# Attention kernel: normalisation of half of the tokens moved from the stretch ahead of the second attention into its first pair

## The chip, the cores and the metric

One core of a Trainium2 chip runs one program. The metric is the device time of one execution in microseconds (us). TensorE's matmuls are called PE here, its weight loads PEld, VectorE is DVE, ScalarE is ACT, GpSimd is POOL, and SP is the engine that issues most DMAs.

## The reference

The input is x, 16 batches of 100 tokens of 256 numbers, and a context of 16 x 361 x 256. Two layers follow each other, each a gated cross attention and a gated mixture of eight experts:

```python
x = x + tanh(g_xattn[0]) * L0_xattn(layernorm(x), ctx, ctx, mask)
x = x + tanh(g_ffn[0])   * L0_ffn(layernorm(x))          # 8 experts, top 2, capacity
x = x + tanh(g_xattn[1]) * L1_xattn(layernorm(x), ctx, ctx, mask)
x = x + tanh(g_ffn[1])   * L1_ffn(layernorm(x))          # 8 experts, top 2
```

`layernorm` is (x - mean) / sqrt(variance + 1e-5) over the 256 numbers of a token. The change concerns the one that stands at the head of the third line: the normalised x is the query input of the second attention (16 heads of 64).

## The kernel before

The program has four stages in a row: the first attention (`a_`), the first experts (`f_`, function `experts_first`), the second attention (`b_`, function `attention_second`), the second experts. x lies in SBUF as 100 partitions x (16 x 256); `T["xn"]` is a second tile of that size, and `T["xn_t"]` the transposed normalised tokens, 128 partitions x 2 x 1600.

**The stretch ahead of the second attention.** The tokens come in four quarters of four batches. For each quarter q the code has these pieces:
- `load_back` (SP): the experts' rows come back by DMA, the first share into xn, the second into `xe` (quarters 0 and 1) or the weight buffer `w` (quarters 2 and 3).
- `scale_second(act, q)` (L1997): ACT multiplies the second share by its weight, four activations of 100x256.
- `combine(dve, q)`: DVE adds the first share times its weight to x (L2006, four instructions), then the second share (L2011), and then calls `centre.average`: four `bn_stats` (L1871) and four `bn_aggr` (L1874).
- `centre.scales(pool, q)`: four small POOL instructions (L1882 to L1885) make 1/sqrt(variance) and the shift.
- `centre.apply(act, q)`: ACT writes the normalised quarter into xn, four activations (L1892).
- `centre.turn(pe, bank, q, k)`: PE transposes it (L1900), four transposes for each of k = 0, 1; `turn_rows(q)` calls it for both, into the score banks.
- `keep_rows(q)`: ACT copies both banks of 400 columns to `xn_t` (L865).

Beside this the stretch makes keys (K), values (V) and queries (Q) of batches 0 and 1 in units, the list `pre`: 8 K, 6 V, 8 Q. A Q unit is two matmuls (L639, each shows as two in the trace), a cast on ACT (L808) and a subtraction on DVE (L898). The Q units of `pre` read only quarter 0 of `xn_t`. Units go through three PSUM banks in turn: unit u waits until unit u-3 has been taken. Before the first pair PE waits for all rows kept, for all memsets (semaphore `zeroed`, the last is POOL's memset of the probability tile) and for all units taken:

```python
            pe.wait_ge(rows_kept, DK * Centre.GROUPS)
            pe.wait_ge(zeroed, 8)
            for k in taken.values():
                pe.wait_ge(k.sem, k.before(k.pre))
            iterations(pe, steps)
```

**The pairs.** `iterations` runs eight pairs of batches; pair 0 is written out ahead of a loop. A pair has eight steps p = 0 to 7 of four heads. In each step PE makes scores for four heads (L698), the transposes of the probabilities of the step before (L708, one PSUM bank that ACT empties at L827), the values product of the step before that (L730), and in between the units of `second_schedule`. DVE takes the four maxima (L960), inverts sums and multiplies (L968, L973), and takes units; ACT does the exponentials (L819), copies (L827) and takes units (L808, L795). DVE, ACT and PE run their own written order, so what an engine does between two heads holds up what is queued behind it.

The schedule has four units of kinds W (output projection, step 2), N (step 5), G (step 6) and C (step 7) that work on the pair before (their last field is -1). In pair 0 there is no pair before: PE passes over them and only counts (`no_outputs`), and DVE calls `count_taken`. Pair i makes the queries of pair i+1, so quarter 1 of `xn_t` is read from pair 1's steps on, and quarters 2 and 3 later still.

SP loads contexts during the pairs; a load waits for POOL's `split_context` (L551, L554) of the context before.

## Time and profile before

| | us |
|---|---|
| median of 3 runs | 1506.0 |
| lowest and highest of them | 1504.61, 1637.23 |
| the profiled execution, its own time | 1506.07 |
| its span, first to last instruction | 1504.3 |
| second attention's eight pairs, from 648 on, about | 592 |
| the stretch 605 to 648 ahead of it | 43 |

A profile row of the timeline reads: start in us from the span's start, length in us, engine, source line, operation, output <- input, shapes, count, and in brackets how long the engine was idle before it and who released it. Where PE is busy all the time, the time is PE's; where it idles, the releaser in the brackets names what was late.

### The profile page before, as it was taken

The numbers are of one execution on the slowest core, as the hardware profiler recorded it, in microseconds if no ns is written. First come the engines' busy times: TensorE is split into PE (matmuls) and PEld (weight loads), VectorE is DVE, ScalarE is ACT, GpSimd is POOL, SyncE is SP. The second block draws the span as 40 slices with busy tenths as digits, with TensorE's granted clock in tenths as the row PEclk, the third lists the DMA queues.
The fourth block names the chain that finished last, engine by engine and source line by source line (L and its number), as shares of the span: only waits on it lengthen the run. The fifth ranks groups of instructions, "written<-read, shape, count | busy, mean of one in ns | idle before, by whom it ended". The sixth has DMA issues, their size and how long they took to land. (4 is left out here: it accounts for less than half of the span.)

```text
span 1504.3 us, 35796 instructions
## 1 busy us (share of the span) xinstructions
PE 1307.0 (87%) x10432; PEld 1022.8 (68%) x10433; DVE 867.5 (58%) x2865; ACT 816.6 (54%) x2244; POOL 450.5 (30%) x826
## 2 busy tenths in 40 slices
PE   5899999998199999799999999999999998369991
PEld 3666666666178888677787878777787786236661
DVE  3666666666246556765666767675766767222223
ACT  3777777777055556565555645464655556023332
POOL 5325555454312424400112121212112122312221
PEclk8999999999589999899999999999999999579996
DMA  8933223220235432400000000000000015111215
GB/s 214 370 129 110 80 84 110 100 68 14 64 128 180 165 114 96 124 12 13 12 13 23 11 23 11 22 11 9 14 11 22 0 40 239 59 37 61 61 57 145
DMA packets 45809, 114.96 MB, mean 76 GB/s; under 512 B 9096, under 2 KB 29256, under 8 KB 42028
## 3 DMA queue, kind: packets, MB, share of 16 engines
q1 hardware_dynamic: 38064, 97.26, 19.8%
q0 software_dynamic: 7168, 14.99, 3.1%
q10 hardware_dynamic: 480, 1.64, 0.4%
q8 instruction: 34, 0.56, 0.2%
q14 instruction: 63, 0.52, 0.1%
HBM read 70.42 MB, written 47.65 MB: 78 GB/s over the span
## 5 line engine op out<-in xcount | busy, mean ns | idle before, releaser
L819 ACT ACTIVATE b_prob<-b_prob,b_low 100x361 f32<-100x361 f32 x256 | 154.9, 605 | 102.3 <-DVE b_low L960 102.3
L827 ACT COPY b_prob_t<-b_ps_t 128x300 f32<-128x300 f32 x256 | 103.6, 405 | 103.2 <-PE b_ps_t L708 99.6
L644 PE MATMUL b_ps_p<-b_context_part,b_wk_part 128*128 128x362 f32 x768 | 158.4, 343 | 0.4 <-DVE b_keys_lo L898 0.4
L1560 ACT ACTIVATE a_prob<-a_prob,a_low 100x361 f32<-100x361 f32 x256 | 153.2, 601 | 0.4 <-DVE a_low L1703 0.4
L650 PE MATMUL b_ps_p<-b_wv_part,b_context_part 128*128 128x512 f32 (+1 forms) x576 | 151.5, 405 | 0.0
L960 DVE CUSTOM_DVE_ANT_0 b_prob<-b_ps_s,b_mask_bias 100x361 f32<-100x361 f32 x256 | 121.1, 530 | 35.3 <-PE b_ps_s L698 20.3
L1568 ACT COPY a_prob_t<-a_ps_t 128x300 f32<-128x300 f32 x256 | 97.5, 406 | 80.0 <-PE a_ps_t L1463 79.7
L1703 DVE CUSTOM_DVE_ANT_0 a_prob<-a_ps_s,a_mask_bias 100x361 f32<-100x361 f32 x256 | 121.4, 531 | 32.7 <-PE a_ps_s L1453 28.8
L708 PE MATMUL b_ps_t<-ident,b_prob 100*128 100x100 f32 x768 | 117.5, 262 | 24.3 <-ACT b_prob_t L827 24.1
L644 PEld LDWEIGHTS b_ps_p<-b_context_part,b_wk_part 128*128 128x128 f32 x768 | 125.0, 190 | 1.2 <-DVE b_keys_lo L898 0.7
L708 PEld LDWEIGHTS b_ps_t<-ident,b_prob 100*128 100x128 f32 x768 | 79.1, 142 | 66.3 <-issue 49.8
L973 DVE TENSOR_SCALAR b_prob<-b_prob,b_inv 100x361 f32<-100x361 f32 x256 | 115.7, 452 | 2.2
L650 PEld LDWEIGHTS b_ps_p<-b_wv_part,b_context_part 128*128 128x128 f32 (+1 forms) x576 | 100.7, 182 | 21.9
L1463 PE MATMUL a_ps_t<-ident,a_prob 100*128 100x100 f32 x768 | 102.1, 257 | 4.1 <-ACT a_prob_t L1568 3.1
L1463 PEld LDWEIGHTS a_ps_t<-ident,a_prob 100*128 100x128 f32 x768 | 79.8, 144 | 36.2 <-issue 23.0
L898 DVE TENSOR_TENSOR b_keys_lo<-b_ps_p,b_keys_hi 128x361 fp32r<-128x361 f32 x128 | 67.9, 532 | 59.9 <-ACT b_keys_hi L808 59.9
L2149 PE MATMUL f_ps<-f_xt,f_w_part 128*128 128x512 f32 x384 | 90.9, 397 | 2.7 <-DVE f_xt L2243 2.7
L2164 PE MATMUL f_ps<-f_w_both,f_ht 128*128 128x512 f32 (+1 forms) x512 | 92.4, 340 | 0.1
L2164 PEld LDWEIGHTS f_ps<-f_w_both,f_ht 128*128 128x128 f32 x512 | 78.4, 188 | 11.9 <-DVE f_ye L2270 0.4
L2149 PEld LDWEIGHTS f_ps<-f_xt,f_w_part 128*128 128x128 f32 x384 | 73.7, 192 | 18.5 <-issue 3.1
L730 PE MATMUL b_ps_s<-b_prob_t,b_values 128*64 128x100 f32 (+1 forms) x1536 | 83.3, 259 | 1.4 <-issue 1.4
L541 POOL TENSOR_SCALAR b_mask_bias<-b_mask_raw 100x361 f32<-100x361 uint8 x16 | 11.7, 731 | 237.5 <-issue 189.1
(302 smaller groups left out, 2731.2 us busy)
## 6 DMA issues: line engine op xcount, KB each, us to landing
rows_in<-zero SPq DMA_DIRECT2D x44, 514.0 KB, 6.1
w<-in_c_fc SPq DMA_DIRECT2D x8, 1024.0 KB, 7.4
w<-in_c_proj SPq DMA_DIRECT2D x8, 1024.0 KB, 6.1
a_context<-in_ctx SPq DMA_DIRECT2D x16, 361.0 KB, 3.6
b_context<-in_ctx SPq DMA_DIRECT2D x16, 361.0 KB
rows_in<-rows_in SPq DMA_DIRECT2D x8, 514.0 KB, 5.0
f_xe<-rows_in SPq DMA_DIRECT2D x8, 514.0 KB, 3.5
f_xe<-rows_in SPq DMA_DIRECT2D x32, 128.5 KB, 2.0
```

The costliest lines, as they stand in the source:

```text
L644: ins = nc.tensor.matmul(bank[:, 0:LN2], w_parts["k"][a][:, k, t * P:(t + 1) * P], cx_parts[s][b][:, k, :], start=m == 0, stop=m == DK * l ...
L650: ins = nc.tensor.matmul(bank[0:kn, :], cx_parts[s][b][:, k, k0:k0 + kn], w_parts["v"][a][:, k, p * 512:(p + 1) * 512], start=m == 0, stop ...
L708: ins = nc.tensor.transpose(ps_t[:, c * S:(c + 1) * S], prob[0:S, k % PAIR_PB, c * P:(c + 1) * P], T["ident"][0:S, 0:S])
L819: nc.scalar.activation(prob[0:S, k, 0:L], prob[0:S, k, 0:L], ACT.Exp, bias=low[0:S, k:k + 1], scale=-1.0, accum_out=total[0:S, k:k + 1]).t ...
L827: nc.scalar.copy(pt[:, k % PAIR_PT, :], ps_t[:, 0:KT_N * S]).then_inc(pt_ready.sem, 1)
L960: nc.vector.tensor_tensor_reduce(out=prob[0:S, k, 0:L], in0=ps_s[g % 4][0:S, 0:L], in1=bias[s][0:S, :], scale=-layer.scale, scalar=BIG, op ...
L973: nc.vector.tensor_scalar(prob[0:S, k, 0:L], prob[0:S, k, 0:L], inv[0:S, k:k + 1], None, ALU.mult).then_inc(normed.sem, 1)
L1463: ins = nc.tensor.transpose(ps_t[k % 2][:, c * S:(c + 1) * S], prob[0:S, k % QUAD_PB, c * P:(c + 1) * P], T["ident"][0:S, 0:S])
L1560: nc.scalar.activation(prob[0:S, k, 0:L], prob[0:S, k, 0:L], ACT.Exp, bias=low[0:S, k:k + 1], scale=-1.0, accum_out=total[0:S, r:r + 1]).t ...
L1703: nc.vector.tensor_tensor_reduce(out=prob[0:S, k, 0:L], in0=ps_s[g % FIRST][0:S, 0:L], in1=bias[s][0:S, :], scale=-layer.scale, scalar=BIG ...
L2149: ins = nc.tensor.matmul(ps[2 + f % 2][:, :], w1_parts[a][:, k, f * P:(f + 1) * P], xt[b][:, k, :], start=m == 0, stop=m == DK * len(PASSE ...
L2164: ins = nc.tensor.matmul(ps[4 + j % 2][:, 0:w * D], ht[a][:, f, j * P:(j + 1) * P], w2_both[:, f, 0:w, :].rearrange("p m d -> p (m d)"), s ...
```

## The change

Only quarters 0 and 1 are normalised ahead of the second attention. For quarters 2 and 3:
- DVE takes their averages at the end of steps 0 and 1 of pair 0; POOL makes their scales at the head of its work for pair 0, ahead of `split_context`; ACT applies them at the end of steps 1 and 3 of pair 0.
- PE transposes them in pair 0 in the unit slots W, N, G and C that it passed over, four transposes in each, into the unit's bank, and DVE copies each to `xn_t`.
- The sums into x (`combine`) of all four quarters stay ahead of pair 0, and POOL waits for them before its last memset, which pair 0 waits for. ACT's `scale_second` of quarters 2 and 3 comes earlier in its order.
- The small tiles of the statistics now lie in tiles that are there already (`top`, `chosen`, `picked`); a tile `gap` of the old size keeps the other addresses.

The first attention only gets its tiles passed in another form. The diff, without that part:

```diff
+    QUARTERS_AHEAD, ROW_TURNS = 2, {"W": (2, 0), "N": (2, 1), "G": (3, 0), "C": (3, 1)}
...
             def steps(i, sched):
+                if i == 0:
+                    for q in range(QUARTERS_AHEAD, Centre.GROUPS):
+                        centre.scales(pool, q)
...
-            for q in range(1, Centre.GROUPS):
+            for q in range(1, QUARTERS_AHEAD):
                 centre.scales(pool, q)
+            experts["summed"](pool)
             pool.memset(prob[:, :, L:KT_N * P], 0.0).then_inc(zeroed, 1)
...
-                elif kind == "none" or no_outputs(i, p):
+                elif kind != "none" and no_outputs(i, p):
+                    ins = centre.turn(pe, bank, *ROW_TURNS[kind])
+                elif kind == "none":
...
             turn_rows(1)
-            turn_rows(2)
-            ahead(FIRST_Q + BANKS, n_pre - 2)
-            turn_rows(3)
-            ahead(n_pre - 2, n_pre)
-            pe.wait_ge(rows_kept, DK * Centre.GROUPS)
+            ahead(FIRST_Q + BANKS, n_pre)
+            pe.wait_ge(rows_kept, DK * QUARTERS_AHEAD)
...
+                    if isinstance(i, int) and i == 0 and p in (1, 3):
+                        centre.apply(act, QUARTERS_AHEAD + p // 2)
...
             centre.apply(act, 0)
+            experts["scale_second"](act, 2)
             keep_rows(0)
-            experts["scale_second"](act, 2)
+            experts["scale_second"](act, 3)
             centre.apply(act, 1)
             take_ahead(FIRST_Q, FIRST_Q + BANKS)
-            experts["scale_second"](act, 3)
             keep_rows(1)
-            centre.apply(act, 2)
-            keep_rows(2)
-            take_ahead(FIRST_Q + BANKS, n_pre - 3)
-            centre.apply(act, 3)
-            take_ahead(n_pre - 3, n_pre - 2)
-            keep_rows(3)
-            take_ahead(n_pre - 2, n_pre)
+            take_ahead(FIRST_Q + BANKS, n_pre)
...
+            def keep_turned_rows(u, kind, i):
+
+                dve.wait_ge(unit_done.sem, unit_done.at(i, u + 1))
+                nc.vector.tensor_copy(centre.place(*ROW_TURNS[kind]), bank_of(u, False)[:, 0:Centre.width]).then_inc(taken["D"].sem, 1)
...
+                    if isinstance(i, int) and i == 0 and p < Centre.GROUPS - QUARTERS_AHEAD:
+                        experts["average"](dve, QUARTERS_AHEAD + p)
...
+    def summed(eng):
+        eng.wait_ge(added, Centre.GROUPS)
```

What stands on ACT in the stretch ahead of the pairs, from the application of quarter 0 (`xn<-x`) to the first exponential's table load; `w_0_1` is the second share of quarters 2 and 3. Before:

```order
L1892 ACTIVATE xn<-x,f_quarter_shift,f_quarter_rs 100x256 x4
L865 COPY xn_t<-b_ps_s 128x400 x2
L1997 ACTIVATE w_0_1<-w_0_1,f_weight 100x256 x4
L1892 ACTIVATE xn<-x,f_quarter_shift,f_quarter_rs 100x256 x4
L808 CAST b_queries_hi<-b_ps_p 128x200 x3
L1997 ACTIVATE w_0_1<-w_0_1,f_weight 100x256 x4
L865 COPY xn_t<-b_ps_s 128x400 x2
L1892 ACTIVATE xn<-x,f_quarter_shift,f_quarter_rs 100x256 x4
L865 COPY xn_t<-b_ps_s 128x400 x2
L808 CAST b_queries_hi<-b_ps_p 128x200 x2
L1892 ACTIVATE xn<-x,f_quarter_shift,f_quarter_rs 100x256 x4
L808 CAST b_queries_hi<-b_ps_p 128x200
```

And after, at the same place:

```order
L1900 ACTIVATE xn<-x,picked 100x256 x4
L2007 ACTIVATE w_0_1<-w_0_1,f_weight 100x256 x4
L871 COPY xn_t<-b_ps_s 128x400 x2
L2007 ACTIVATE w_0_1<-w_0_1,f_weight 100x256 x4
L1900 ACTIVATE xn<-x,picked 100x256 x4
L812 CAST b_queries_hi<-b_ps_p 128x200 x3
L871 COPY xn_t<-b_ps_s 128x400 x2
L812 CAST b_queries_hi<-b_ps_p 128x200 x5
L823 ACT_TABLE_LOAD
```

Two applications and two pairs of copies have left the stretch, and both weightings stand ahead of the second application.

On PE at the same place, from the transposes of quarter 0 to the first scores of pair 0. Before:

```order
L1900 MATMUL b_ps_s<-ident,xn 128x100 x8
L639 MATMUL b_ps_p<-xn_t,wq 128x200 x6
L1900 MATMUL b_ps_s<-ident,xn 128x100 x16
L639 MATMUL b_ps_p<-xn_t,wq 128x200 x6
L1900 MATMUL b_ps_s<-ident,xn 128x100 x8
L639 MATMUL b_ps_p<-xn_t,wq 128x200 x4
L698 MATMUL b_ps_s<-b_keys_hi,b_queries_hi 100x362 x2
```

After:

```order
L1908 MATMUL b_ps_s<-ident,xn 128x100 x8
L644 MATMUL b_ps_p<-xn_t,wq 128x200 x6
L1908 MATMUL b_ps_s<-ident,xn 128x100 x8
L644 MATMUL b_ps_p<-xn_t,wq 128x200 x10
L705 MATMUL b_ps_s<-b_keys_hi,b_queries_hi 100x362 x2
```

Sixteen of the 32 transposes are gone from it, and the last five Q units (ten matmuls) stand in one piece.

On DVE at the end of step 0 of pair 0, between the last multiplication of that step and the first maximum of step 1 (the maxima are the rows `ISA`), after the change:

```order
L975 RECIPROCAL b_inv<-b_total 100x1
L980 TENSOR_SCALAR b_prob<-b_prob,b_inv 100x361
L1879 BN_STATS top<-x 100x6 x4
L1882 BN_AGGR chosen<-top 100x2 x4
L967 ISA b_prob,b_low<-b_ps_s,b_mask_bias 100x361
```

Before, the two rows of the statistics are not there, and the maximum follows the multiplication. The same two rows stand at the end of step 1.

## Rows read from the trace of the kernel before

**Rows 1.** Busy time by stage: window, its length, then each engine, granted clock, DMA share, GB/s

```profile
605.00:648.00 43.00, 31.63 (x154) 27.81 (x153) 29.51 (x74) 27.03 (x61) 15.55 (x26) 0.84 0.36 93
648.00:1240.00 592.00, 566.09 (x4552) 462.32 (x4552) 396.61 (x1460) 325.61 (x946) 113.12 (x221) 1.00 0.06 16
```

**Rows 2.** Waits, 605 to 648: who waited for whom, us in total, times, longest

```profile
PE b_ps_s L1900 <- ACT xn L1892: 9.3, 3, 4.8
```

**Rows 3.** Timeline of all engines, 616 to 648

```profile
623.68 2.07 ACT L1892 ACTIVATE xn<-x,f_quarter_shift,f_quarter_rs 100x256 f32<-100x256 f32 x4 [0.21 <-POOL f_quarter_shift L1885]
...
625.81 1.59 PE L1900 MATMUL b_ps_s<-ident,xn 100*128 100x100 f32 x8 [2.96 <-ACT xn L1892]
...
627.83 1.70 ACT L1997 ACTIVATE w<-w,f_weight 100x256 f32<-100x256 f32 x4
...
627.99 4.37 PE L639 MATMUL b_ps_p<-xn_t,wq 128*128 128x200 f32 x12 [0.58 <-ACT xn_t L865]
628.72 0.27 POOL L1885 TENSOR_TENSOR f_quarter_shift<-f_quarter_shift,f_quarter_rs 100x4 f32<-100x4 f32 x1
...
629.57 1.22 DVE L2011 TENSOR_TENSOR x<-x,w 100x1024 f32<-100x1024 f32 x1 [0.64 <-ACT w L1997]
630.83 1.41 DVE L1871 BATCH_NORM_STATS2 f_quarter_st<-x 100x6 f32<-100x256 f32 x4
...
632.15 0.92 PE L1900 MATMUL b_ps_s<-ident,xn 100*128 100x100 f32 x8
...
632.56 1.65 DVE L2006 SCALAR_TENSOR_TENSOR x<-xn,f_weight,x 100x256 f32<-100x256 f32 x4
...
634.22 0.87 ACT L865 COPY xn_t<-b_ps_s 128x400 f32<-128x400 f32 x2
...
637.35 0.88 DVE L898 TENSOR_TENSOR b_queries_lo<-b_ps_p,b_queries_hi 128x200 fp32r<-128x200 f32 x3
...
645.36 1.54 PE L639 MATMUL b_ps_p<-xn_t,wq 128*128 128x200 f32 x8
...
647.92 0.41 PE L698 MATMUL b_ps_s<-b_keys_hi,b_queries_hi 64*100 64x362 f32 x2 [1.02 <-DVE b_queries_lo L898]
```

**Rows 4.** Busy time in stretches of 1 us, columns as in rows 1

```profile
625.00:626.00 1.00, 0.19 (x1) 0.19 (x2) 1.00 (x4) 0.76 (x2) 0.87 (x3) 0.73 0.05 8
...
632.00:633.00 1.00, 1.00 (x10) 0.78 (x8) 0.97 (x7) 0.61 (x2) 0.27 (x1) 0.86 0.00 0
...
635.00:636.00 1.00, 0.00 (x0) 0.00 (x0) 0.97 (x3) 0.42 (x2) 0.64 (x1) 0.85 0.00 0
```

**Rows 5.** Timeline of all engines, steps 0 to 2 of pair 0

```profile
653.33 0.53 DVE L960 CUSTOM_DVE_ANT_0 b_prob<-b_ps_s,b_mask_bias 100x361 f32<-100x361 f32 x1
...
655.03 0.45 PE L708 MATMUL b_ps_t<-ident,b_prob 100*128 100x100 f32 x3 [0.92 <-ACT b_prob_t L827]
...
656.34 0.42 PE L708 MATMUL b_ps_t<-ident,b_prob 100*128 100x100 f32 x3
...
656.55 1.65 PE L650 MATMUL b_ps_p<-b_wv_part,b_context_part 128*128 128x512 f32 x6
...
659.92 0.59 ACT L795 COPY b_values<-b_ps_p 128x512 f32<-128x512 f32 x1 [1.02 <-PE b_ps_p L650]
...
660.78 0.54 DVE L960 CUSTOM_DVE_ANT_0 b_prob<-b_ps_s,b_mask_bias 100x361 f32<-100x361 f32 x1 [1.35 <-PE b_ps_s L698]
...
661.95 0.39 ACT L827 COPY b_prob_t<-b_ps_t 128x300 f32<-128x300 f32 x1
...
662.49 0.45 PE L708 MATMUL b_ps_t<-ident,b_prob 100*128 100x100 f32 x3
```

**Rows 6.** Timeline of ACT: first exponential of step 4 of pair 0

```profile
676.12 0.60 ACT L819 ACTIVATE b_prob<-b_prob,b_low 100x361 f32<-100x361 f32 x1 [1.92 <-DVE b_low L960]
```

**Rows 7.** Groups by line, 648 to 1240: busy us, mean ns, idle before

```profile
L235 DVE COPY b_rows_t<-b_ps_p 128x400 f32<-128x400 f32 x6 | 3.4, 575 | 5.9 <-PE b_ps_p L230 5.9
...
L819 ACT ACT_TABLE_LOAD x1 | 1.3, 1283 | 0.0
```

More of the change, by code:

```diff
@@ L912, in take_outputs @@
                     dve_own.skip(dve, 2)
-                    count_taken(sched, u, i)
+                    keep_turned_rows(u, kind, i)
                     return
@@ L930, in take @@
                     take_outputs(u, unit, sched, i)
-                elif unit[0] == "none" or (unit[0] in "NGC" and no_outputs(i, unit[3])):
+                elif unit[0] == "none":
                     count_taken(sched, u, i)
+                elif unit[0] in "NGC" and no_outputs(i, unit[3]):
+                    keep_turned_rows(u, unit[0], i)
                 elif unit[0] in "NGC":
@@ L1034, in _ @@
             take_ahead(0, FIRST_V + 1)
-            experts["combine"](dve, 0)
-            take_ahead(FIRST_V + 1, FIRST_V + 4)
-            experts["combine"](dve, 1)
-            take_ahead(FIRST_V + 4, FIRST_Q)
-            experts["combine"](dve, 2)
-            experts["combine"](dve, 3)
+            for q, values in ((0, 4), (1, 6)):
+                experts["combine"](dve, q)
+                experts["average"](dve, q)
+                take_ahead(FIRST_V + (1, 4)[q], FIRST_V + values)
+            for q in range(QUARTERS_AHEAD, Centre.GROUPS):
+                experts["combine"](dve, q)
             take_ahead(FIRST_Q, n_pre)
@@ L1165, in attention_first @@
     pre_at = list(enumerate(pre.units))
-    centre = Centre(nc, T, nm, sb, T["x"])
+    centre = Centre(nc, T, nm, (sb("quarter_st", [P, B, 6]), sb("quarter_mv", [P, B, 2]), sb("quarter_rs", [P, B]), sb("quarter_shift", [P, B])), T["x"])
     quarter_turned = nc.alloc_semaphore(nm + "quarter_turned")
@@ L1856, with __init__ @@
     width = PER * S
-    def __init__(self, nc, T, nm, sb, src):
+    def __init__(self, nc, T, nm, tiles, src):
         self.nc, self.T, self.src = nc, T, src
-        self.st, self.mv = sb("quarter_st", [P, B, 6]), sb("quarter_mv", [P, B, 2])
-        self.rs, self.shift = sb("quarter_rs", [P, B]), sb("quarter_shift", [P, B])
+        self.st, self.mv, self.rs, self.shift = tiles
         self.own, self.pool_own = Chain(nc, nm + "quarter_own"), Chain(nc, nm + "quarter_pool_own")
@@ L1923, in experts_first @@
     WIDTH = WIDE[0]
+    sb("gap", [P, B, 10])
     ps = [ctx.enter_context(nc.psum_tensor(f"{nm}ps{k}", [P, 512], F32)) for k in range(8)]
@@ L1958, in experts_first @@
     QUARTER = Centre.PER * D
-    centre = Centre(nc, T, nm, sb, T["x"])
+    centre = Centre(nc, T, nm, (top[:, :, 0:6], chosen[:, :, :].rearrange("p k b -> p (k b)").rearrange("p (b t) -> p b t", t=2),
+                                picked[:, 0, :], picked[:, 1, :]), T["x"])
     w1, w2 = T["w1_0"], T["w2_0"]
@@ L2011, in combine, with average @@
         nc.vector.tensor_tensor(x, x, back(1, q), ALU.add).then_inc(added, 1)
+    def average(dve, q):
         dve.wait_ge(added, q + 1)
@@ L2303, in experts_first @@
     return dict(sync=sync, gpsimd=gpsimd, tensor=tensor, scalar=scalar, vector=vector, load_back=load_back, sent=sent,
-                scale_second=scale_second, combine=combine, centre=centre, first_weights_split=first_weights_split,
+                scale_second=scale_second, combine=combine, average=average, summed=summed, centre=centre, first_weights_split=first_weights_split,
                 second_weights_split=second_weights_split, rows_split=rows_split, weighted=weighted,
```

## The prediction

> **What bounds the kernel now.** I read the busy time by stage first. In the eight pairs from 648 on PE is busy 566.1 of 592.0 us at the full clock; in the 43 us ahead of them it is busy 31.6 us only, and the mean granted clock is 0.84 [rows 1]. So a microsecond of PE work or of PE waiting inside the pairs costs a microsecond, while the stretch ahead of them is a chain over four engines, worth what its last wait says. Second, the waits of that stretch: PE's largest is for ACT's application of the norm (xn), 9.3 us in three waits, the longest 4.8 [rows 2]. Third, the timeline: PE's first scores of pair 0 start at 647.92, 1.02 us after the last query matmul has ended at 645.36 + 1.54 = 646.90 [rows 3]. What goes out of this chain moves 647.92, and only that counts there. A measurement of this kernel can tell about 2% (30 us) from no change; all that follows is smaller.
>
> **What goes: the start of pair 0.** I build the new chain from the durations of rows 3, in the new order.
> - ACT ends the application of quarter 0 at 623.68 + 2.07 = 625.75. Now the weighting of quarter 2 follows, 1.70, to 627.45; PE's transposes of quarter 0 end at 625.81 + 1.59 = 627.40, so the two copies follow at once, 0.87, to 628.3. The first Q unit starts at about 628.4, where it started at 627.99: 0.4 later.
> - ACT goes on with the weighting of quarter 3 to 630.0 and the application of quarter 1, 2.07, to 632.1. Its scales from POOL are ready at 628.72 + 0.27 = 628.99, so nothing waits for them.
> - PE's first three Q units took 627.99 to 632.15; they now end at about 632.5. The transposes of quarter 1 follow, 0.92, to 633.4.
> - DVE ended the first part of quarter 2's sum at 629.57 - 0.64 = 628.93 and then waited for ACT's weighting. That wait goes. The rest: 1.22, then 1.65 and 1.22 for quarter 3, to 633.1 with the small gaps. The eight instructions of statistics behind each sum are gone. The subtraction of the first Q unit (0.88 for three, 0.3 each) ends at about 633.5, and this frees the bank of the fourth.
> - The five last Q units start at 633.6. Two took 1.54, so five take 3.85, to 637.45, and with the 1.02 behind them the first scores start at 638.5.
>
> The start moves from 647.92 to 638.5: -9.4 us. POOL's last memset now waits for the sums at 633.1, and PE for it, but it is done four microseconds before 638.5. The loads of the shares need no new time: they were issued early, and in the 1 us at 625 DMA moves almost nothing (share 0.05, rows 4). Bounds: if the five units ran at half the clock, as the first three did (4.37 for three, 1.46 each), they would take 7.3 and the gain would be 6.0; if each small gap closed, about 10.2.
>
> **What comes in pair 0.** Here PE has no slack to absorb it, so for each item I ask what idle time covers it.
> - *Averages of quarter 2, end of step 0, DVE.* Four `bn_stats` and four `bn_aggr` took 632.56 - 630.83 = 1.75 rounded [rows 3]. They stand ahead of the first maximum of step 1 at 653.33, which has no idle time before it; ACT waits for that maximum, copies the transposes, and PE waits 0.92 for ACT at 655.03 [rows 5]. All of it reaches PE: +1.75. Between 0 and 1.75.
> - *Application of quarter 2, end of step 1, ACT, 2.07.* ACT ends a copy at 659.92 + 0.59 = 660.5, the application ends at 662.55, then an exponential of 0.6, and the copy that stood at 661.95 stands at 663.15, 1.2 later. PE's next transposes at 662.49 need it, and it ended at 662.34, 0.15 before [rows 5]. So +1.0; between 0 and 2.07.
> - *Averages of quarter 3, end of step 1, DVE, 1.75.* 1.35 of it falls into idle time at 660.78 [rows 5]; the other 0.4 lies beside ACT's application of quarter 2. 0; between 0 and 1.75.
> - *Application of quarter 3, end of step 3, ACT.* The exponential behind it had 1.92 idle before it [rows 6], against 2.07: +0.15; between 0 and 2.07.
> - *Sixteen transposes on PE, in four groups.* Three take 656.55 - 656.34 = 0.21 to the next matmul [rows 5], so four 0.28; from the other side eight took 0.92, so four 0.46 [rows 3]. 1.1 to 1.8, I take 1.2 since the pitch is what counts on a full PE.
> - *Four DVE copies of 400 columns.* The same copy in later pairs takes 0.575 [rows 7], 2.3 in all. The first stands ahead of the release of an output bank in step 2, the others in steps with DVE idle time of a microsecond and more. Between 0 and 2.3; I take 1.0.
> - *POOL and SP.* The scales of both quarters stand ahead of `split_context`, which therefore waits for the averages at the end of step 1, two steps later than now, and with it one context load on SP. A step is 592 / 64 = 9.25 us [rows 1], so it ends about 19 us into the pair; the split context is first read in step 4, from 37 us on: nothing. PE is queued behind none of these.
> - *No table load.* ACT's application is an Identity activation among exponentials. The loop's pairs have such activations too, and there is one table load in 592 us [rows 7]; none is added.
>
> **The sum.** -9.4 + 1.75 + 1.0 + 0.15 + 1.2 + 1.0 = -4.3 us. The profiled execution took 1506.07 for a span of 1504.3, so I forecast 1501.8 for a like one; the median shown, 1506.0, is 0.07 lower, which gives 1501.7.
>
> **Rivals.**
> - *A: pair 0 covers nearly all.* If the application of quarter 2 and the four copies are covered, as ACT's 1.02 idle time at 659.92 and DVE's 1.35 at 660.78 would suggest [rows 5], there stay 1.75 + 1.2: -9.4 + 2.95 = -6.4, 1499.6. Against it: the copy at 661.95 has only 0.15 of slack to PE.
> - *B: the clock.* PE stood idle 2.96 us before 625.81 and in the 1 us at 625 the granted clock is 0.73, on its way to half; in the 1 us at 632 it is back (0.86), after PE had been busy almost without a break from 627.99; at 635, with PE idle since 633.07, it falls again (0.85) [rows 3, 4]. A low period thus lasted about 6.5 us. After the change PE's idle time in step 1 grows to 0.92 + 1.75 = 2.7 us, nearly as long as the first of these. If the clock falls there, 6.5 us run at 1.2 instead of 2.4 GHz and lose half: +3.3, 1505.0. The same +3.4 comes if the clock isn't back before the last five Q units (7.3 instead of 3.85). For it: the length of the gap. Against it: the gap of 2.96 is longer, and the 1.02 us before 647.92 had no such effect.
> - The Trainium skill (TensorE: Matmul & The Clock Gate, section "What's actually happening") says that the throttled state is the default and that activity releases it, that is, an idle PE drops to half its clock and must work for a while to get it back. By that rule B is right wherever a gap is long enough. The trace agrees with both directions; that the gap of pair 0 is long enough no row shows.
> - *C: slower, since the ring of PE, ACT and DVE in pair 0 has no slack.* Each head goes PE, DVE, ACT, DVE, PE, ACT in a fixed order, with one bank for the transposes. If every added microsecond of any engine comes back to PE, the price is 2 x 1.75 + 2 x 2.07 + 4 x 0.575 + 1.2 = 11.1 against 9.4: +1.7, 1507.8. It decides from the point where the additions to pair 0 exceed 9.4. For it: the place at 653.33 behaves so. Against it: the idle times of 1.35 and 1.92 that rows 5 and 6 show.
> - *D: the change doesn't do what it says*, because something else holds the start: the sums now gate it through POOL. Their chain ends at 633.1, so it would have to slip by five microseconds; I give it no chance of its own.
>
> **How the numbers follow.** Forecast 0.55, A 0.2, B 0.15, C 0.1. The range goes from A's time less a microsecond for the difference between executions (1504.61 and 1506.0 are two of the three runs) to somewhat short of C: 1498.6 to 1507.0. The sum of bounds would allow -10.2 + 1.1 = -9.1 and -6.0 + 11.7 = +5.7; neither end is likely, as all items would have to stand at one side. No case reaches 2% either way: within 2% 0.98, and one in a hundred on either side for a median that disturbed runs have shifted, as one run of 1637.23 shows can happen.
>
> **What would show it.** In the changed profile: scores of pair 0 (L705 there) start near 638.5, and no idle time of PE of 4.8 us before them; DVE's second wait for ACT's weighting is gone; in step 1 of pair 0 an idle time of PE of about 2.7 us before the transposes, released by ACT's copy; in step 2 about 1 us before the second transposes; no table load beside the first exponential; granted clock 1.00 over pair 0. Pairs 1 to 7 as long as now. I am wrong in the first term if the scores start after 641, wrong in the second if pair 0 grows by less than 3 or by more than 7 us, and B is right if the clock in pair 0 is below 1.00.

## The result and the profile after

The changed kernel takes 1500.52 us in the median of 16 runs (1494.69 to 1504.38); beside it the kernel before takes 1505.34 (16 runs, 1499.77 to 1637.23). The ratio is 0.9965, with a 95% interval of 0.9949 to 0.9981: about 5 us less, no difference by the measure of 2%. The ratio leaves out the run of 1637.23, which fell in a slower state that some executions show whatever the kernel. The forecast was 1501.7, with a range of 1498.6 to 1507.0. The profiled execution took 1497.83 us, its span is 1496.1.

The busy time by stage, the columns those of [rows 1]; the pairs now start at 638:

```profile
605.00:638.00 33.00, 27.46 (x137) 23.93 (x136) 25.99 (x58) 21.11 (x49) 10.46 (x17) 0.90 0.48 121
638.00:1233.00 595.00, 568.46 (x4585) 464.48 (x4586) 402.50 (x1490) 331.31 (x961) 117.92 (x232) 1.00 0.06 16
```

Ten of the 43 us ahead of the pairs are gone, and the stretch of the pairs, cut at round figures, is 3 us longer. The waits of 605 to 638; the first row answers to [rows 2], the second was not there:

```profile
PE b_ps_s L1908 <- ACT xn L1900: 3.0, 1, 3.0
...
POOL b_prob L609 <- DVE x L2021: 4.2, 1, 4.2
```

PE waits for the norm once instead of three times. The timeline of that stretch, which answers to [rows 3]:

```profile
623.44 2.08 ACT L1900 ACTIVATE xn<-x,picked 100x256 f32<-100x256 f32 x4 [0.21 <-POOL picked L1893]
...
627.77 1.71 ACT L2007 ACTIVATE w<-w,f_weight 100x256 f32<-100x256 f32 x4
...
627.92 4.27 PE L644 MATMUL b_ps_p<-xn_t,wq 128*128 128x200 f32 x12 [0.76 <-ACT xn_t L871]
...
629.38 2.07 ACT L1900 ACTIVATE xn<-x,picked 100x256 f32<-100x256 f32 x4
...
631.70 1.23 DVE L2021 TENSOR_TENSOR x<-x,w 100x1024 f32<-100x1024 f32 x1
...
632.03 0.85 PE L1908 MATMUL b_ps_s<-ident,xn 100*128 100x100 f32 x8
...
632.99 0.25 POOL L609 MEMSET b_prob<- 128x184 f32 x1 [4.25 <-DVE x L2021]
...
633.26 3.65 PE L644 MATMUL b_ps_p<-xn_t,wq 128*128 128x200 f32 x20 [0.37 <-DVE b_queries_lo L898]
...
637.93 0.41 PE L705 MATMUL b_ps_s<-b_keys_hi,b_queries_hi 64*100 64x362 f32 x2 [1.02 <-DVE b_queries_lo L898]
```

The last row is the first of the scores: 637.93 against 647.92. In the first steps of pair 0, which answer to [rows 5]:

```profile
643.34 1.40 DVE L1879 BATCH_NORM_STATS2 top<-x 100x6 f32<-100x256 f32 x4
...
646.74 0.45 PE L715 MATMUL b_ps_t<-ident,b_prob 100*128 100x100 f32 x3 [2.62 <-ACT b_prob_t L831]
...
652.08 2.08 ACT L1900 ACTIVATE xn<-x,picked 100x256 f32<-100x256 f32 x4
...
655.18 0.45 PE L715 MATMUL b_ps_t<-ident,b_prob 100*128 100x100 f32 x3 [1.00 <-ACT b_prob_t L831]
...
656.75 0.51 PE L1908 MATMUL b_ps_p<-ident,xn 100*128 100x100 f32 x4
657.19 1.26 PE L737 MATMUL b_ps_s<-b_prob_t,b_values 128*64 128x100 f32 x24
...
658.59 0.55 DVE L910 COPY xn_t<-b_ps_p 128x400 f32<-128x400 f32 x1
```

PE waits 2.62 us in step 1, released by ACT's copy behind DVE's averages, and 1.00 in step 2, behind ACT's application. Where the time went in the profiled executions: the scores start 9.99 us earlier. The first output projection of pair 0, in its step 6, starts at 697.16 after and at 703.80 before, so from the first scores on to there it takes 59.24 us instead of 55.87, 3.37 more, and the growth stays 3.36 up to the first transposes of pair 1. Start and pair 0 together give -6.6 us. The rest of the 8.2 us between the two executions, 1.6, came later, and it is a net of differences on both sides that executions of one kernel show too. From the projection of pair 0 to the one at 1196.08 (1188.30 after) after was 1.14 us shorter, with the full clock in both. Then before had a stretch of low clock of 3.4 us, from 1205.7, which after has not: 1.6 us. Behind the pairs, where after was 1.2 us longer, it had low clock for 17.1 us from 1263.4, and before for 10.2 from 1277.4. No table load was added: one of 1.28 us at 637.29, as before at 647.28. The medians say 5 us.

### The profile page after: what moved, and what is told of

The parts are those of the page before. It is cut to its first block, busy times and chain, and to the rows that moved or that the text cites. A ratio compares the mean times of both kernels' runs of the same rounds, so it can differ in the third digit from the quotient of the medians.

```text
span 1496.1 us, 35788 instructions
## 1 busy us (share of the span) xinstructions
PE 1305.1 (87%) x10432; PEld 1020.6 (68%) x10433; DVE 867.8 (58%) x2869; ACT 814.0 (54%) x2240; POOL 450.1 (30%) x826
## 3 DMA queue, kind: packets, MB, share of 16 engines
q0 software_dynamic: 7168, 14.99, 3.1%
## 4 chain that ended last, share of the span: by engine, by line
PE 57%; DVE 5%; issue 5%; DMA 2%; ACT 2%; POOL 1%; DVEq 0%; ACTq 0%; SPq 0%; POOLq 0%
PE b_ps_p L655 8%; PE b_ps_p L649 7%; PE f_ps L2176 6%; PE f_ps L2161 6%; PE b_ps_t L715 6%; PE b_ps_s L737 5%; PE f_ps L2533 4%; PE b_ps_p L676 4%; PE f_ps L2549 4%; PE b_ps_s L705 3%; PE b_ps_p L644 3%; PE f_ps L2541 1%; ACT b_prob_t L831 1%; DMA w<-by_token 1%; PE f_ps L2151 1%
## 5 line engine op out<-in xcount | busy, mean ns | idle before, releaser
L649 PE MATMUL b_ps_p<-b_context_part,b_wk_part 128*128 128x362 f32 x768 | 157.7, 342 | 0.4 <-DVE b_keys_lo L898 0.4
L649 PEld LDWEIGHTS b_ps_p<-b_context_part,b_wk_part 128*128 128x128 f32 x768 | 124.4, 189 | 1.3 <-DVE b_keys_lo L898 0.7
L737 PEld LDWEIGHTS b_ps_s<-b_prob_t,b_values 128*64 128x64 f32 (+1 forms) x1536 | 70.7, 140 | 16.7 <-issue 15.9
```

The costliest lines, as they stand in the source:

```text
L649: ins = nc.tensor.matmul(bank[:, 0:LN2], w_parts["k"][a][:, k, t * P:(t + 1) * P], cx_parts[s][b][:, k, :], start=m == 0, stop=m == DK * l ...
L737: ins = nc.tensor.matmul(ps_o[g][64 * e:64 * e + 64, :], vt[b][0:kn, c, h * 64:h * 64 + 64], pt[0:kn, (2 * t + e) % PAIR_PT, c * S:(c + 1) ...
```

## The experiments

On some chips the first attention ends 22 to 30 us later in the traces, that of the kernel before as well (its medians are 1505 to 1506 us on some chips and 1531 on others), so times of a single run are compared only with those of the same chip, and most readings go by distances in the traces:
- A: from the start of ACT's application of quarter 0 ahead of the pairs to the first scores of pair 0;
- B: from the first scores to the second group of probability transposes, the ones at 655.03 in [rows 5] (in step 1);
- C: from the first scores to the transposes at 662.49 in [rows 5] (in step 2);
- D: from the first scores to the first output projection of pair 0, the one at 703.80 before (in step 6). The expectation of e8 calls it that of pair 1, but what it multiplies is the first batch of pair 0. The transposes in the slots W, N and G lie within D, those of C (704.50 after) behind it.

| kernel | A | B | C | D | lower clock in the first 15 us of pair 0 |
|---|---|---|---|---|---|
| before | 24.24 | 7.10 | 14.56 | 55.87 | none |
| changed | 14.49 | 8.81 | 17.25 | 59.24 | none |
| e1_weighting_early | 23.65 | 7.11 | 14.54 | 55.83 | none |
| e2_averages_ahead | 21.02 | 7.11 | 15.55 | 57.52 | none |
| e3_both_in_step_0 | 14.48 | 10.51 | 20.33 | 62.32 | 3.4 us |
| e4_old_act_order | 17.46 | 8.81 | 17.25 | 59.23 | none |
| changed_again | 14.48 | 8.82 | 20.07 | 62.06 | 6.8 us |
| e5_short_row_copies | 14.49 | 8.81 | 18.82 | 60.66 | 3.4 us |
| e6_stats_between_casts | 14.48 | 7.11 | 15.55 | 57.52 | none |
| e7_applied_in_halves | 14.49 | 7.10 | 14.82 | 57.34 | none |
| e8_split_before_scales_of_fourth | 14.49 | 7.25 | 14.96 | 56.93 | none |
| e9_changed_split_first | 14.49 | 8.81 | 17.26 | 59.23 | none |
| changed_beside_best | 14.49 | 8.81 | 17.25 | 59.22 | none |
| best_beside_changed | 14.50 | 7.26 | 14.99 | 57.00 | none |

**ACT's order alone.** The kernel before, with both weightings ahead of the application of quarter 1:

```diff
             centre.apply(act, 0)
+            experts["scale_second"](act, 2)
             keep_rows(0)
-            experts["scale_second"](act, 2)
+            experts["scale_second"](act, 3)
             centre.apply(act, 1)
             take_ahead(FIRST_Q, FIRST_Q + BANKS)
-            experts["scale_second"](act, 3)
```

> The kernel before with one part of the change alone: ACT weighs quarter 2 ahead of the copies of quarter 0, and quarter 3 ahead of the application of quarter 1. Theory (the chain of the four quarters sets the start of pair 0, so the order is worth only the 0.64 us that DVE waited for the weighting): the first scores of pair 0 start 0.6 us earlier than before, at 647.3, and PE still waits about 4.8 and 1.5 us for the applications of quarters 2 and 3. Rival (a good part of the 10 us comes from the order of the weightings, not from what was moved away): the first scores start before 645.

A is 23.65 instead of 24.24: 0.59 less, as the theory says, and nothing else moves. With four quarters ahead of the pairs the order of ACT is worth 0.6 of the 9.75 us of A.

**The order taken back.** The changed kernel with ACT's order of before:

> The changed kernel with ACT's order of the kernel before for what is left ahead of pair 0: copies of quarter 0, weighting of quarter 2, application of quarter 1, three query casts, weighting of quarter 3, copies of quarter 1. Theory (after the change the sums are last, so the weightings' place matters now): DVE's last sum waits for the weighting of quarter 3 and ends 2.5 us later, and the first scores start at 640.6. Rival (the order matters as little as in the kernel before): 637.9 to 638.5.

A is 17.46, 2.97 more than changed. DVE waits for the weighting again and ends the sums later, and the banks of the last five Q units come free later:

```profile
660.35 1.71 ACT L2007 ACTIVATE w<-w,f_weight 100x256 f32<-100x256 f32 x4
...
662.09 1.23 DVE L2021 TENSOR_TENSOR x<-x,w 100x1024 f32<-100x1024 f32 x1 [1.55 <-ACT w L2007]
...
663.65 5.18 PE L644 MATMUL b_ps_p<-xn_t,wq 128*128 128x200 f32 x20 [2.85 <-DVE b_queries_lo L898]
```

But only half of the 2.97 is the order. From the start of the application of quarter 0 to the end of the sums it is 10.93 us here (652.39 to 663.32) and 9.49 in the changed kernel (623.44 to 632.93), 1.44 more, and so much later the twenty matmuls of the last five Q units start. The other 1.53 is the clock: PE waits 2.85 us for them, the granted clock falls to 1.2 GHz from 663.4 to 666.8, and they take 5.18 us instead of 3.65. The expectation put the later end of the sums at 2.5 us and did not think of the clock; that the start came out near it is chance.

The same edit is worth 0.6 us by itself and 1.4 together with the rest, and in this execution as much again in clock: with four quarters the wait for the norm of quarters 2 and 3 ended the chain, with two of them the sums do.

**Averages left ahead of the pairs.** `average` of quarters 2 and 3 right behind their sums, and none in pair 0:

```diff
             for q in range(QUARTERS_AHEAD, Centre.GROUPS):
                 experts["combine"](dve, q)
+                experts["average"](dve, q)
...
-                    if isinstance(i, int) and i == 0 and p < Centre.GROUPS - QUARTERS_AHEAD:
-                        experts["average"](dve, QUARTERS_AHEAD + p)
```

> The changed kernel with the averages of quarters 2 and 3 back ahead of pair 0; scales, applications and transposes stay in pair 0. Theory (DVE's chain of sums sets the start, and what DVE does at the end of step 0 reaches PE whole): the first scores start 3.5 us later than in the changed kernel (637.9), at 641.4, and PE's idle time in step 1 falls from 2.62 to 0.92; the first output projection of pair 0 comes 3.5 - 1.7 = 1.8 later than 697.16. Rival (the sums' chain has slack, since the five last queries wait for ACT): the scores start at 638 to 639, and the projection comes earlier than 697.16.

D is 57.52, 1.72 less than changed, and B is that of before: in pair 0 the averages cost what was forecast (1.75), and those of quarter 3 nothing. A is 21.02, 6.53 more where the expectation had the 3.5 of DVE's statistics alone. Of the rest 2.9 is the clock. PE waits 3.74 us for DVE, and most of the stretch behind it runs at 1.2 GHz (granted so from 663.3 to 670.1):

```profile
664.26 6.54 PE L644 MATMUL b_ps_p<-xn_t,wq 128*128 128x200 f32 x20 [3.74 <-DVE b_queries_lo L898]
```

```profile
662.00:663.00 1.00, 0.00 (x0) 0.00 (x0) 0.96 (x4) 0.00 (x0) 0.68 (x3) 1.00 0.00 0
663.00:664.00 1.00, 0.00 (x0) 0.00 (x0) 0.97 (x7) 0.00 (x0) 0.92 (x2) 0.66 0.00 0
664.00:665.00 1.00, 0.74 (x2) 0.74 (x3) 0.75 (x3) 0.00 (x0) 0.77 (x4) 0.50 0.00 0
```

The second fence is in stretches of 1 us, its columns as in [rows 1]. The same twenty matmuls take 3.65 us in the changed kernel (the row at 633.26 above). Before had the like: its second stretch of low clock, from 635.7 to 642.5, begins 2.6 us after PE has run dry in its wait of 4.8 us and reaches 4.6 us beyond it; after the change it is gone. The row of before at the end of that wait:

```profile
637.89 1.56 PE L1900 MATMUL b_ps_s<-ident,xn 100*128 100x100 f32 x8 [4.82 <-ACT xn L1892]
```

Stretches of 1 us of before, and then of after:

```profile
636.00:637.00 1.00, 0.00 (x0) 0.00 (x0) 1.00 (x4) 1.00 (x3) 0.00 (x0) 0.50 0.00 0
...
640.00:641.00 1.00, 1.00 (x5) 1.00 (x4) 0.00 (x0) 0.13 (x1) 0.00 (x0) 0.50 0.00 0
```

```profile
632.00:633.00 1.00, 0.89 (x9) 0.66 (x7) 1.00 (x2) 0.74 (x3) 0.01 (x1) 1.00 0.00 0
...
635.00:636.00 1.00, 1.00 (x8) 1.00 (x7) 0.41 (x2) 0.57 (x2) 0.00 (x0) 1.00 0.00 0
```

**Both averages in step 0.** This makes the wait of step 1 longer:

```diff
-                    if isinstance(i, int) and i == 0 and p < Centre.GROUPS - QUARTERS_AHEAD:
-                        experts["average"](dve, QUARTERS_AHEAD + p)
+                    if isinstance(i, int) and i == 0 and p == 0:
+                        experts["average"](dve, QUARTERS_AHEAD)
+                        experts["average"](dve, QUARTERS_AHEAD + 1)
```

> The changed kernel with the averages of both quarters at the end of step 0. PE's idle time in step 1 should be 2.62 + 1.75 = 4.4 us. Theory of the clock (rival B of the prediction, with a gap that is long enough): the granted clock falls to 1.2 GHz in or right after this gap and stays there for some 6.5 us, so pair 0's first output projection comes 1.75 + 3.3 = 5 us later than 697.16. Rival (the gap costs only itself): 1.75 later, 698.9, at full clock throughout.

PE waits 4.32 us in step 1, B is 1.70 more than changed, so DVE's work there goes to PE one for one. Behind the wait the clock is at 1.2 GHz for 3.4 us, and D is 3.08 more: 1.70 of wait and 1.38 of clock. The theory was right that the clock falls, but it stays low for half of the 6.5 us expected, so the total lies between the two, nearer to the rival's.

**The changed kernel once more**, for whether the clock falls in its own pair 0.

> The changed kernel itself once more, as the measure for the next three on the same chip. From the start of ACT's application of quarter 0 to the first scores of pair 0 it should take 14.5 us (24.2 in the kernel before), from these scores to the first output projection of pair 0 59.2 (55.9 before).

The median is 1526.66 (12 runs), of before 1530.77 (21 runs), ratio 0.9978 (0.9959 to 0.9996). In this execution the clock does fall at the wait of 2.62 us, from 673.2, in its last part, to 680.0. The transposes and the stretches of 1 us around them:

```profile
673.88 0.73 PE L715 MATMUL b_ps_t<-ident,b_prob 100*128 100x100 f32 x3 [2.62 <-ACT b_prob_t L831]
674.31 2.16 PE L649 MATMUL b_ps_p<-b_context_part,b_wk_part 128*128 128x362 f32 x6
```

```profile
672.00:673.00 1.00, 0.00 (x0) 0.00 (x0) 1.00 (x7) 0.25 (x1) 0.46 (x2) 1.00 0.00 0
673.00:674.00 1.00, 0.12 (x1) 0.15 (x2) 1.00 (x7) 1.00 (x4) 0.94 (x1) 0.58 0.00 0
...
679.00:680.00 1.00, 1.00 (x6) 0.80 (x5) 0.39 (x1) 0.00 (x0) 0.00 (x0) 0.50 0.03 8
680.00:681.00 1.00, 1.00 (x6) 0.82 (x6) 1.00 (x4) 0.41 (x1) 0.00 (x0) 1.00 0.00 0
```

The six matmuls of L649 take 2.16 us, where in the profiled run of the result they take 1.24. C and D are 2.82 more. With e5, where the fall comes 1.2 us behind the wait, this is two of the six profiled executions that have the wait of 2.62 us in step 1 (one of the three of the changed kernel itself); the other four kept the full clock. None of the seven traces of the versions that have 0.92 to 1.07 us there shows it in pair 0.

**The copies almost taken out.** Each of the four copies of quarters 2 and 3 takes 8 columns instead of 400 (0.15 us each instead of about 0.55); the other columns of those rows are left out of the computation.

```diff
-                nc.vector.tensor_copy(centre.place(*ROW_TURNS[kind]), bank_of(u, False)[:, 0:Centre.width]).then_inc(taken["D"].sem, 1)
+                nc.vector.tensor_copy(centre.place(*ROW_TURNS[kind])[:, 0:8], bank_of(u, False)[:, 0:8]).then_inc(taken["D"].sem, 1)
```

> The changed kernel with DVE's four copies of the transposed rows cut from 400 columns to 8, so most queries of batches 8 to 15 are made from rows that were never written. The prediction charged these copies 1.0 us. Theory after the result: DVE had idle time for all but some 0.1 of it; scores to first output projection 59.1 us. Rival (the prediction's charge is right and something else was too dear): 58.2 to 58.5.

The clock fell in this execution too, for 3.4 us, within B to C, so the copies are read from behind it: C to D is 60.66 - 18.82 = 41.84 us against 59.24 - 17.25 = 41.99. The 392 columns taken out of each copy cost 0.15 us in all, not the 1.0 forecast for the copies.

**The averages of quarter 2 between the last subtractions.** In the stretch ahead of the pairs DVE waits for ACT's casts between the last Q units, 0.31 to 0.85 us each time. `stats_of` is one `bn_stats`, `aggregate` the four `bn_aggr` of a quarter:

```diff
-                    if isinstance(i, int) and i == 0 and p < Centre.GROUPS - QUARTERS_AHEAD:
-                        experts["average"](dve, QUARTERS_AHEAD + p)
+                    if isinstance(i, int) and i == 0 and p == 1:
+                        experts["average"](dve, QUARTERS_AHEAD + 1)
...
-            take_ahead(FIRST_Q, n_pre)
+            take_ahead(FIRST_Q, FIRST_Q + BANKS)
...
+            for b in (stats, stats + 1):
+                mark = centre.stats_of(b)
+            take_ahead(FIRST_Q + 3, FIRST_Q + 4)
+            mark = centre.stats_of(stats + 2)
+            take_ahead(FIRST_Q + 4, FIRST_Q + 5)
+            mark = centre.stats_of(stats + 3)
+            take_ahead(FIRST_Q + 5, FIRST_Q + 6)
+            centre.aggregate(dve, QUARTERS_AHEAD, mark)
+            take_ahead(FIRST_Q + 6, n_pre)
```

> The changed kernel with the average of quarter 2 taken apart and put between DVE's subtractions of the last five queries ahead of pair 0, where DVE waits 0.3 to 0.85 us for each cast. Theory (these gaps hold it, and it costs 1.7 where it stands now): 14.5 us to the first scores as before this edit, PE's idle time in step 1 falls from 2.62 to 0.92, and scores to first output projection takes 57.5 instead of 59.2. Rival (the subtractions then come late and hold PE's banks): the 1.7 comes back ahead of the scores, 16 us to them.

A stays 14.48, B is 7.11 and D 57.52: the 1.72 us are saved and nothing is paid for them, as the theory says.

**And the applications in halves.** Two of a quarter's four activations at the end of each of steps 0 to 3, instead of four at the end of steps 1 and 3:

```diff
-                    if isinstance(i, int) and i == 0 and p in (1, 3):
-                        centre.apply(act, QUARTERS_AHEAD + p // 2)
+                    if isinstance(i, int) and i == 0 and p < 4:
+                        centre.apply_half(act, QUARTERS_AHEAD + p // 2, p % 2)
```

> As the kernel with the average between the casts, and ACT's application of quarters 2 and 3 cut into halves of two activations, at the ends of steps 0, 1, 2 and 3. Theory (ACT idles 1.34 us at the end of step 0 and 0.85 at that of step 1, so each half of 1.05 is nearly covered): the second transposes of step 2 no longer wait 1.0 us; scores to first output projection 56.5 to 56.8, in all 2.5 us less than the changed kernel up to that point. Rival (DVE's average of quarter 3, so far hidden beside the application, comes out with 0.4 or more): 57.0 to 57.4.

The median is 1523.37 (10 runs) against 1530.77 of before on the same chip, ratio 0.9955 (0.9938 to 0.9972). C is 0.73 less than in e6, but D only 0.18, since PE now waits in step 3. That number falls into the rival's range, though not for the rival's reason, DVE's averages: it is a multiply of DVE. The timeline there, DVE, POOL and PE:

```profile
676.54 1.04 DVE L980 TENSOR_SCALAR b_prob<-b_prob,b_inv 100x361 f32<-100x361 f32 x1
676.59 0.79 POOL L552 CAST b_context_part<-b_context 128x722 fp32r<-128x722 f32 x1
...
677.56 1.60 POOL L555 TENSOR_TENSOR b_context_part<-b_context,b_context_part 128x722 fp32r<-128x722 f32 x1 [0.18 <-POOL b_context_part L552]
...
678.00 1.36 DVE L980 TENSOR_SCALAR b_prob<-b_prob,b_inv 100x361 f32<-100x361 f32 x1
...
679.79 0.40 DVE L980 TENSOR_SCALAR b_prob<-b_prob,b_inv 100x361 f32<-100x361 f32 x1
...
681.21 0.41 PE L705 MATMUL b_ps_s<-b_keys_hi,b_queries_hi 64*100 64x362 f32 x2 [0.63 <-DVE b_out_t L992]
```

The multiply takes 0.40 us in most places and here 1.04 and 1.36, each ending 0.2 us after one of the two instructions of POOL's `split_context`.

**`split_context` back where it was.** In e8 the scales of quarter 3 go behind it; in e9, from the changed kernel, the scales of both quarters do. The edit of e8:

```diff
                 if i == 0:
-                    for q in range(QUARTERS_AHEAD, Centre.GROUPS):
-                        centre.scales(pool, q)
+                    centre.scales(pool, QUARTERS_AHEAD)
                 if sched is full:

                     split_context(0, i + 2, unit_done.at(i, 0))
+                if i == 0:
+                    centre.scales(pool, QUARTERS_AHEAD + 1)
+                if sched is full:
                     convert(0, i + 2, maxed.at(i, H))
```

> The version before it (averages of quarter 2 beside the casts, application in halves), with one change of order on POOL: the scales of quarter 2, then split_context, then the scales of quarter 3. Theory: the multiplies of 1.04 and 1.36 us in step 2 of pair 0 are long because split_context runs beside them; with split_context back at about 647 to 650 us after the start of the trace of before (right behind the first scores), they take 0.40 us, PE's wait of 0.63 us for DVE's output copy ahead of the scores of step 3 goes, and from the first scores to the first output projection of pair 1 it takes 56.6 to 56.9 us instead of 57.3. Rival: the multiplies are long for another reason (the keys' subtractions beside them, or the bank): they stay above 0.6 us and the distance stays at 57.3. The time: about 0.5 us less than that version's 1523.4, so 7 to 8 us below the kernel before, ratio 0.995.

> The changed kernel with one change of order on POOL alone: split_context first, then the scales of quarters 2 and 3. Theory: split_context starts within 1 us of the first scores, the multiplies of step 1 of pair 0 take 0.40 us instead of 0.82 and 0.66, the application of quarter 2 still starts behind step 1's units (its scales are made 5 us before), and pair 0 is at most 0.3 us shorter, since those multiplies stood ahead of no wait of PE there: first scores to second transposes of step 1 8.8, of step 2 17.0 to 17.3, to the first output projection 59.0 to 59.2 where the clock stays up (2.8 more where it falls in step 1). Rival: the multiplies stay long, because the bank or the casts slow them, not POOL.

The multiplies of the same place. First e8:

```profile
639.06 0.79 POOL L552 CAST b_context_part<-b_context 128x722 fp32r<-128x722 f32 x1
...
641.29 0.55 DVE L982 TENSOR_SCALAR b_prob<-b_prob,b_inv 100x361 f32<-100x361 f32 x1
...
653.62 0.41 DVE L982 TENSOR_SCALAR b_prob<-b_prob,b_inv 100x361 f32<-100x361 f32 x1
...
655.06 0.40 DVE L982 TENSOR_SCALAR b_prob<-b_prob,b_inv 100x361 f32<-100x361 f32 x1
```

And the changed kernel, where they took 0.82 and 0.66 (in e9 0.41 and 0.40):

```profile
654.97 0.82 DVE L980 TENSOR_SCALAR b_prob<-b_prob,b_inv 100x361 f32<-100x361 f32 x1
...
656.92 0.66 DVE L980 TENSOR_SCALAR b_prob<-b_prob,b_inv 100x361 f32<-100x361 f32 x1
```

In e8 the multiplies are short again and D is 56.93, 0.41 less than in e7, although one multiply in step 0, at 641.29, now meets the tail of `split_context` and B is 0.15 more. In e9 they are short too, and D is 59.23 as before the edit: in the changed kernel the long multiplies stood ahead of nothing that PE waited for. The median of e8 is 1495.89 (6 runs) against 1505.79 of before (11 runs), ratio 0.9939 (0.9919 to 0.9959).

**That version beside the changed kernel**, in the same rounds on one chip.

> The changed kernel as it is, timed in the same rounds as the version of the next run. About 5 us below the kernel before (ratio 0.9965, seen so far 0.9965 and 0.9978). Its pair 0 either keeps the full clock (59.2 us from first scores to the first output projection) or falls for a few us after the wait of 2.6 us in step 1 (60.7 to 62.1).

> The version with the averages of quarter 2 beside the casts, the application in halves and split_context ahead of the scales of quarter 3. Theory: 59.2 - 56.9 = 2.3 us less than the changed kernel where that keeps its clock in pair 0, up to 5 us less where it does not, so 2.3 to 5 us below the changed kernel's median and 8 to 10 below the kernel before. Rival: its earlier gain of 9.9 us over the kernel before was chance of the clock elsewhere in the program, and beside the changed kernel it shows less than 2 us.

| | median us | runs | lowest, highest | ratio to before, 95% |
|---|---|---|---|---|
| before | 1531.22 | 23 | 1525.48, 1534.91 | |
| changed | 1524.44 | 12 | 1520.15, 1529.48 | 0.9964 (0.9947 to 0.9981) |
| e8's version | 1524.74 | 12 | 1518.57, 1528.90 | 0.9961 (0.9945 to 0.9978) |

The medians come out as the rival says, but they don't refute the theory. Pair 0 is 2.2 us shorter in the traces (D 57.00 against 59.22), yet the medians don't differ. Executions of one kernel spread over 9 to 10 us here, and twelve of them don't resolve two. The profiled executions show what fills the spread: the first scores start at 663.48 in e8's version and at 659.98 in the changed one, which comes from stages ahead of the change, and the clock falls for 3.4 us at 810.2 in pair 1 in the one and not in the other. The 9.9 us of e8 over before, 6.5 here, are probably in part such luck; no run separates it.

## Why the prediction was right

The median, 1500.5, lies 1.2 us below the forecast, 0.9 above rival A's time and inside the range. Every step was off by less than a microsecond, but all to the same side: the traces give -9.99 + 3.37 = -6.6 us where the sum gave -4.3. That the medians say -4.8, nearer to the forecast than to this, is in part luck: their interval reaches from -7.7 to -2.9 us and can't tell -6.6 from -4.3, executions in which the clock falls in pair 0 count in it, and the rest of the program differs from run to run by as much.
- *The start of pair 0*, forecast -9.4 (638.5): -9.99 (637.93). The chain ran as built: no wait before the second weighting, the application of quarter 1 from 629.38, the sums' end at 631.70 + 1.23 = 632.93 (forecast 633.1), five Q units in 3.65 (3.85), 1.02 us behind them. Of the difference 0.24 is an earlier start of the application of quarter 0. Runs e1 and e4 confirm the step on the weighting: its early place is worth 0.6 us with four quarters ahead and 1.4 once quarters 2 and 3 have left, to which the clock can add 1.5 (e4).
- *What the step gave no reason for*: the clock. It took the last units at the full pitch from the row at 645.36 [rows 3], and had half the clock as a bound and in rival B. The pitch was right; what it rests on is that the wait of 4.8 us is gone and with it the low clock around its end. e2 puts a wait of 3.74 us back and the same twenty matmuls take 6.54 instead of 3.65; e4 puts one of 2.85 back and they take 5.18. How much of the 9.99 us is clock in this way no run separates.
- *POOL's memset behind the sums*: as forecast, done at 633.24, 4.7 us before the first scores; that is the answer to rival D.
- *Averages of quarter 2*, +1.75: +1.71 (B 8.81 against 7.10), and e2 and e6 take just this away. The wait is 2.62, forecast 2.7.
- *Application of quarter 2*, +1.0: +0.98, the rest of C (2.69 - 1.71). e7 takes 0.73 of it away.
- *Averages of quarter 3*, 0: in e2 and e6, which differ in where these stand, C and D are the same. The forecast holds.
- *Application of quarter 3*, *transposes* and *copies*, 0.15 + 1.2 + 1.0 = 2.35: from C on the changed kernel loses 41.99 - 41.31 = 0.68. These are the terms that were mis-sized. I follow the growth of the distance from the first scores, after less before, from one instruction of PE to the next. At the group of transposes in slot W (656.75) it goes from 2.67 to 2.95, at the one in N (687.69) from 3.10 to 3.12, where PE of before had been idle for 0.26 us, at the one in G (692.12) from 3.12 to 3.37, and at the one in C (704.50) it doesn't move, since PE waits there either way (0.59 us before, 0.25 after). So the transposes cost 0.55 us, not 1.2. Of the copies only the first shows, 0.15 at the scores of step 3, which is what e5 gives for them. The application of quarter 3, from 667.17 to 669.25, leaves the growth at 3.08: it costs nothing. The premise that PE has no slack, read from [rows 1], is an average (566 of 592 us); in these places it isn't so.
- *POOL and SP*, nothing: right for the time of the changed kernel (e9), but the argument looked at who waits for `split_context` and not at who works beside it. In e7 the same order costs 0.4 us of D (57.34 against 56.93 in e8).
- *The sum*: the start -10.0 instead of -9.4, pair 0 +3.4 instead of +5.1.
- *Rival B*: it is not another case beside the forecast, it is one of two forms of the same kernel: two of the six executions with the wait of 2.62 us have it, for 1.6 us (e5) and 2.8 us (changed_again). The forecast for it was +3.3. *A* is nearest to the profiled pair 0 (+2.95 against +3.37) and to the -6.6 of the traces (-6.4), but for another reason: it let the application of quarter 2 be covered, which costs its full 1.0, and charged 1.2 for the transposes, which cost 0.55. *C* falls: the averages and the application of quarter 3 and three of the four copies don't come back to PE.

## What to carry to other kernels

Work moved into a stretch where one engine is busy 95% of the time costs its full length where it stands between two waits of that engine's ring, as the averages at the head of a step do, and almost nothing at places with slack; the average over the stretch doesn't tell the two apart, the idle time ahead of the waiting instruction does. A gain ahead of such a stretch has to be worked out with the clock that the removed wait had cost, and a wait of 2.6 us newly made can cost the clock in some executions and not in others. When an edit is timed, the length of the same matmuls in both traces tells what part of the difference is clock: in e4 it was half. When an order changes on GpSimd, look for the VectorE instructions that will run beside it, not only for those that wait for it.

## What was not expected of the hardware

- DVE's multiply of 100x361 (SBUF to SBUF, float32) takes 0.40 us, and in pair 0 from 0.55 to 1.36 beside POOL's cast and subtraction, ending 0.2 us after the one or the other. The subtractions and maxima of DVE that read PSUM kept their time beside the same POOL instructions (the four maxima of step 0 in e8, from 639.28 to 641.1, 0.53 each, and the subtraction at 677.57 in e7, 0.51). The kernel before has such multiplies too, in the later pairs: 16 of its 256 take over 0.45 us (1.55 at 763.08), and in no trace is there a long one without POOL at work beside it. The Trainium skill (SBUF — State Buffer, section "SBUF: two separate sides") states that VectorE and GpSimd share a pair of ports as an exclusive lock, for VectorE operations in a two-port mode, or with two inputs in SBUF against a GpSimd operation that reads SBUF, and that the later one is blocked whole. The traces agree in the main: the multiply ends when POOL's instruction has, and where it starts 0.27 us ahead of the cast it keeps its 0.41 (before, at 679.20). But in e7 the multiply of 1.04 us is recorded 0.05 us ahead of the cast, and a small instruction of POOL on `b_dev` that began 0.38 us ahead of the multiply and ended 0.04 us behind it left it at 0.40 (before, at 749.55). Whether this multiply is in one of the modes named no run shows.
- The clock falls at a wait of 2.62 us in two of six executions and not in the others, and stays at 1.2 GHz for 3.4 us in one and 6.8 in the other, with the same instructions in the same distances. A shorter wait can be followed by it too: in pairs 1 to 7 the fourteen traces have 24 stretches of 3.4 us at 1.2 GHz, 20 of them beginning 1.1 to 2.4 us behind a wait of PE of 1.08 us and 4 at one of 1.7 to 1.8; 64 more waits of 1.08 us there are followed by none. The stretch of before from 1205.7 is one of the 20:

```profile
1203.37 0.45 PE L708 MATMUL b_ps_t<-ident,b_prob 100*128 100x100 f32 x3 [1.08 <-ACT b_prob_t L827]
```

The Trainium skill (TensorE: Matmul & The Clock Gate, section "What's actually happening") says that the number of slow matmuls at a kernel's start varies from run to run with the same program; here the like shows in the middle of one. What decides it in an execution no run here shows.
